# Second attention of a two-layer gated cross-attention kernel: bfloat16 maxima transposed after the value product, max rows written by DMA, parts of the next batch moved two half units ahead, sums copied by ScalarE

## What is computed

```
v = values.reshape(N, -1, HEADS, HEAD) @ Wv.T
k = keys.reshape(N, Lk, HEADS, HEAD) @ Wk.T
q = queries.reshape(N, Lq, HEADS, HEAD) @ Wq.T
energy = jnp.einsum('bqhd,bkhd->bhqk', q, k)
energy = jnp.where(mask, energy, jnp.float32(-1e+20))
attn = jax.nn.softmax(energy / np.sqrt(HEAD), axis=-1)
out = jnp.einsum('bhqk,bkhd->bqhd', attn, v).reshape(N, Lq, EMBED)
return out @ Wo.T + bo
x = x + jnp.tanh(g_xattn[1]) * _L1_xattn_ref(ctx_1024, ctx_1024, _layernorm(x, axis=-1), ...)
```

## Time and profile before

| what | value |
|---|---|
| median of three runs | 1420.08 us |
| the profiled execution's own time | 1424.06 us |
| its span, first to last instruction | 1422.3 us |
| TensorE busy | 1264.7 us, 89% |
| VectorE busy | 1044.8 us, 73% |
| ScalarE busy | 854.3 us, 60% |
| GpSimd busy | 160.5 us, 11% |
| second attention, first max product to last transposes | about 231.9 to 453 us |

### The profile page before, as it was taken

The page is one execution under the profiler, slowest core; times in us unless marked ns, Lnnn a source line. Parts: engine busy times, 40 slices in busy tenths (PEclk is TensorE's granted clock), DMA queues, the critical chain, the costliest instruction groups (busy, mean ns, idle before and its releaser), DMA issues.

```text
span 1422.3 us, 26541 instructions
## 1 busy us (share of the span) xinstructions
PE 1264.7 (89%) x10690; PEld 590.5 (42%) x10690; DVE 1044.8 (73%) x1563; ACT 854.3 (60%) x1432; POOL 160.5 (11%) x139
## 2 busy tenths in 40 slices
PE   4898974899899899948899999999999999999988
PEld 3566662454455755514433233232322333233237
DVE  4897494666664756545699999999999999999802
ACT  2233472666665155511287877887887787887871
POOL 2220021110600223310600000000000000000000
PEclk8977985999999999978799999999999999999999
DMA  5000026444450013340524443323443323443003
GB/s 177 24 1 14 1 29 111 95 85 89 90 90 2 0 67 133 134 94 11 82 50 69 82 79 57 75 54 64 82 81 62 67 56 63 82 81 48 2 1 118
DMA packets 78825, 92.56 MB, mean 65 GB/s; under 512 B 15210, under 2 KB 53356, under 8 KB 78704
## 3 DMA queue, kind: packets, MB, share of 16 engines
q1 hardware_dynamic: 78704, 90.87, 31.6%
HBM read 67.02 MB, written 23.80 MB: 64 GB/s over the span
## 4 chain that ended last, share of the span: by engine, by line
PE 58%; DVE 28%; ACT 7%; issue 4%; DMA 1%; SPq 1%; POOL 1%; DVEq 0%; ACTq 0%; POOLq 0%
DVE sm L1971 18%; PE ps L1460 9%; PE ps L1451 8%; PE ps L1432 6%; PE ps L1351 4%; ACT W L964 3%; PE ps L1216 2%; PE ps L1250 2%; PE ps L1570 2%; PE ps L1167 2%; PE ps L1358 2%; PE ps L1241 2%; PE ps L1299 1%; PE ps L1442 1%; PE ps L1387 1%
## 5 line engine op out<-in xcount | busy, mean ns | idle before, releaser
L1971 DVE TENSOR_REDUCE sm<-ps 128x1 f32<-128x1024 f32 x512 | 599.8, 1218 | 33.1 <-PE ps L1432 29.8
L964 ACT ACTIVATE W<-ps 128x512 f32<-128x512 f32 x1024 | 534.8, 604 | 140.2 <-PE ps L1460 136.3
L1460 PE MATMUL ps<-R 99*32 99x512 bf16 x4096 | 318.5, 383 | 6.2 <-ACT W L964 3.2
L1451 PE MATMUL ps<-W,R 128*32 128x512 f32 x2048 | 266.4, 596 | 0.7 <-ACT W L964 0.7
L1460 PEld LDWEIGHTS ps<-R 99*32 99x32 bf16 x4096 | 86.2, 94 | 225.4 <-ACT W L964 168.5
L882 ACT CAST R<-ps 4x2048 bf16<-4x2048 f32 x32 | 59.5, 1858 | 80.7 <-PE ps L1216 80.7
L1776 DVE TENSOR_REDUCE small<-ps 128x4 f32<-128x308 f32 x128 | 60.9, 477 | 62.6 <-PE ps L1205 62.2
L1432 PE MATMUL ps<-R 50*128 50x512 bf16 x512 | 89.2, 389 | 15.6 <-DVE sm L1971 12.9
L1432 PE MATMUL ps<-KM,R 50*128 50x512 bf16 x512 | 87.2, 384 | 9.6 <-DVE sm L1971 6.6
L1451 PEld LDWEIGHTS ps<-W,R 128*32 128x32 f32 x2048 | 63.2, 111 | 42.5 <-ACT W L964 1.4
L765 POOL COPY R<-R 128x512 f32<-128x512 f32 x16 | 10.3, 644 | 591.7 <-PE ps L1451 591.7
(11 more groups left out here) (258 smaller groups left out, 1587.1 us busy)
## 6 DMA issues: line engine op xcount, KB each, us to landing
R<-x_parts SPq DMA_DIRECT2D x96, 128.0 KB, 4.8
R<-q_parts SPq DMA_DIRECT2D x192, 64.0 KB
R<-q_parts SPq DMA_DIRECT2D x96, 128.0 KB
R<-k_parts SPq DMA_DIRECT2D x96, 128.0 KB
x_parts<-R SPq DMA_DIRECT2D x8, 768.0 KB, 4.1
q_parts<-R SPq DMA_DIRECT2D x24, 256.0 KB, 2.6
k_parts<-R SPq DMA_DIRECT2D x24, 256.0 KB, 2.6
X<-in_x SPq DMA_DIRECT2D x4, 1024.0 KB, 9.8
```

The costliest lines, as they stand in the source:

```text
L964: act.activation(PR[:, s % 2, h, :], third_bank("score", 64 * u + n), ACT.Exp, scale=0.25).then_inc(s_sfree, 1)
L1451: mm = pe.matmul(bank(7)[32 * h:32 * h + 32, :], VST[j][:, k, h, :], PR[:, s % 2, h, :], start=(k == 0), stop=(k == TB - 1))
L1460: mm = pe.matmul(o[32 * c:32 * c + 32, :], KST[j][0:MAX_ROW + 1, h, t:t + 32], QST[j][0:MAX_ROW + 1, h, 512 * (s // 8):512 * (s // 8) + 51 ...
L1971: dve.tensor_reduce(MX[:, half, h, q:q + 1], bank(2 * ((p + 1) % 2), 2), AX, ALU.max).then_inc(s_tfree, 1)
```

## The change

- `Mn` is bfloat16, and its transposes use the bfloat16 identity.
- In TensorE's order `max_transposes1(m + 2)` comes ahead of `out_transposes1(m - 2)`.
- The stack has one max row in place of four (97 rows). `K1s` has ones there, set by one memset in place of four copies from the identity. ScalarE copies the 4 x 512 maxima once, into a small buffer `mrow1` of two places, waits for that copy, and issues four DMAs, one for each head, that move one row of 512 bfloat16 each from `mrow1` into the stack. TensorE waits for these DMAs in place of the copy.
- `copy_out1` moves from VectorE's list to ScalarE's, behind the exponentials of the half unit.
- Part halves 8 to 11 are made in half units 6 to 9, and 12 to 15 in 14 to 17. The layer norm chunks before them move with them.

```diff
@@ -202,12 +202,13 @@
         XP = nc.dram_tensor("x_parts", (3, C, T), BF16).ap()
         KXP = nc.dram_tensor("ctx_key_parts", (3, C, B * KX), BF16).ap()
 
-        SR1 = SR + 4
+        SR1 = SR + 1
         K1s = R2f[0:SR1, 0:2464].bitcast(BF16).rearrange("p (h n) -> p h n", h=H)
         V1a = R2f[0:KX, 2464:4512].rearrange("p (b h d) -> p b h d", b=B, h=H)
         mb1 = R2f[0:KX, 4512:5024].bitcast(BF16)
         M1u = R2f[0:KX, 5024:5280].bitcast(U8)
         I4 = R2f[0:KX, 5280:5434].bitcast(BF16)
+        mrow1 = R2f[SR:SR + 4, 5434:5946].bitcast(BF16).rearrange("p (u n) -> p u n", u=2)
         Oe = R2f[:, 6100:7124].rearrange("p (u n) -> p u n", u=2)
         k1T = R5[:, 0:616].rearrange("p (j n) -> p j n", j=2)
         kr1 = R5[:, 616:1232].rearrange("p (j n) -> p j n", j=2)
@@ -220,7 +221,7 @@
         On = R1[:, :].rearrange("p (i c) -> p i c", i=NT)
         OnT = R3f[:, 0:2048].rearrange("p (u j n) -> p u j n", u=2, j=2)
         M1 = small[:, 400:464].rearrange("p (u q j) -> p u q j", u=2, q=8)
-        Mn = small[:, 464:528].rearrange("p (u q j) -> p u q j", u=2, q=8)
+        Mn = small[:, 464:496].bitcast(BF16).rearrange("p (u q j) -> p u q j", u=2, q=8)
         rc1 = small[:, 528:544].rearrange("p (q j) -> p q j", q=4)
         s_w1 = sem("layer1_weights_loaded")
         s_bd = sem("block_diagonals_made")
@@ -245,6 +246,7 @@
         s_mn = sem("max1_negated")
         s_mt = sem("max1_transposed")
         s_mrc = sem("max1_rows")
+        s_mrl = [sem(f"max1_rows_loaded{n}") for n in range(2)]
         s_sc = sem("scores1")
         s_e1 = sem("probs1")
         s_pv = sem("values1_product")
@@ -265,8 +267,11 @@
 
         FIRST = 4
 
+        HALVES = {max(0, 8 * (i // 4) - 2) + i % 4: FIRST + i for i in range(12)}
+        CHUNKS = {0: 3, 4: 4, 6: 5, 12: 6, 14: 7}
+
         def half_in(m):
-            return FIRST + 4 * (m // 8) + m % 8 if m % 8 < 4 and m // 8 + 1 < B else None
+            return HALVES.get(m)
 
         TURNS1 = []
         for m in range(2 * UNITS):
@@ -877,10 +882,21 @@
 
             def max_rows1(m):
                 act.wait_ge(s_mt, m + 1)
+                if m >= 2:
+                    act.wait_ge(s_mrl[m % 2], 64 * (m // 2))
+                act.copy(mrow1[:, m % 2], bank(2)[SR:SR + 4, :]).then_inc(s_mrc, 1)
                 if m >= 6:
                     act.wait_ge(s_sc, 4 * (m - 5))
-                act.copy(Xs[m // 2 % 3][SR:SR1, :, 512 * (m % 2):512 * (m % 2) + 512],
-                         bank(2)[SR:SR1, :].unsqueeze(1).to_broadcast([4, 4, 512])).then_inc(s_mrc, 1)
+                act.wait_ge(s_mrc, m + 1)
+                for j in range(4):
+                    act.dma_start(Xs[m // 2 % 3][SR:SR1, j, 512 * (m % 2):512 * (m % 2) + 512],
+                                  mrow1[j:j + 1, m % 2]).then_inc(s_mrl[m % 2], 16)
+
+            def copy_out1(m):
+                act.wait_ge(s_pv, m + 1)
+                if m >= 2:
+                    act.wait_ge(s_ot1, m - 1)
+                act.copy(Oe[:, m % 2], bank(7)).then_inc(s_oc, 1)
 
             max_rows1(0)
             max_rows1(1)
@@ -894,8 +910,11 @@
                     act.wait_ge(s_sc, n + 1)
                     act.activation(P1[:, m % 2, j, :], bank_of("score", n)[0:KX, :], ACT.Exp,
                                    scale=0.25).then_inc(s_e1, 1)
+                if m >= 1:
+                    copy_out1(m - 1)
                 if m + 2 < 2 * UNITS:
                     max_rows1(m + 2)
+            copy_out1(2 * UNITS - 1)
 
             for c in range(NC):
                 act.wait_ge(s_onT, c + 1)
@@ -1213,8 +1232,8 @@
                     pe.wait_ge(s_mrc, m)
                 for i in range(4):
 
-                    mm = pe.matmul(bank(2)[SR:SR1, P * i:P * i + P], Mn[:, m // 2 % 2, 4 * (m % 2) + i, :],
-                                   identF[:, :], start=True, stop=True)
+                    mm = pe.matmul(bank(2)[SR:SR + 4, P * i:P * i + P], Mn[:, m // 2 % 2, 4 * (m % 2) + i, :],
+                                   identB[:, :], start=True, stop=True)
                 mm.then_inc(s_mt, 1)
 
             def take_bank(what, n):
@@ -1230,7 +1249,7 @@
                 if half_in(m) is not None:
                     transpose_half(half_in(m), take_bank("half", half_in(m)))
                 b, hg = u // 4, u % 4
-                pe.wait_ge(s_mrc, m + 1)
+                pe.wait_ge(s_mrl[m % 2], 64 * (m // 2 + 1))
                 for j in range(4):
                     n = 4 * m + j
                     if u + 1 < UNITS:
@@ -1267,10 +1286,10 @@
                 scores1(m)
                 if m >= 1:
                     values1(m - 1)
+                if m + 2 < 2 * UNITS:
+                    max_transposes1(m + 2)
                 if m >= 2:
                     out_transposes1(m - 2)
-                if m + 2 < 2 * UNITS:
-                    max_transposes1(m + 2)
             values1(2 * UNITS - 1)
             out_transposes1(2 * UNITS - 2)
             out_transposes1(2 * UNITS - 1)
@@ -1763,10 +1782,7 @@
             dve.tensor_copy(I4.rearrange("p (j n) -> p j n", j=4),
                             identB[0:KX, 0:KX].unsqueeze(1).to_broadcast([KX, 4, KX])).then_inc(s_mk1, 1)
 
-            for g in range(4):
-                sel = dve.tensor_copy(K1s[SR:SR1, 4 * g:4 * g + 4, :],
-                                      identB[SR:SR1, SR:SR1].unsqueeze(2).to_broadcast([4, 4, B * KX]))
-            sel.then_inc(s_mk1, 1)
+            dve.memset(K1s[SR:SR1, :, :], 1.0).then_inc(s_mk1, 1)
             ln_chunks(2, [2], lambda c: None)
 
             def reduce1(u, qs):
@@ -1800,27 +1816,16 @@
                 dve.tensor_tensor(dst.rearrange("p q (j d) -> p q j d", j=4), O[:, :, :, 0:D],
                                   rc1.unsqueeze(3).to_broadcast([P, 4, 4, D]), ALU.mult).then_inc(s_on, 1)
 
-            def copy_out1(m):
-                dve.wait_ge(s_pv, m + 1)
-                if m >= 2:
-                    dve.wait_ge(s_ot1, m - 1)
-                dve.tensor_copy(Oe[:, m % 2], bank(7)).then_inc(s_oc, 1)
-
             maxima1(0)
             maxima1(1)
             for m in range(2 * UNITS):
                 n = half_in(m)
                 if m + 2 < 2 * UNITS:
                     maxima1(m + 2, lambda: residue(n, bank_of("half", n)) if n is not None else None)
-                if m >= 1:
-                    copy_out1(m - 1)
-
-                c = 2 * (m // 8) + {0: 3, 6: 4}.get(m % 8, NC)
-                if c < NC:
-                    ln_chunks(2, [c], lambda c: None)
+                if m in CHUNKS:
+                    ln_chunks(2, [CHUNKS[m]], lambda c: None)
                 if m >= 2:
                     normalise1(m - 2)
-            copy_out1(2 * UNITS - 1)
             normalise1(2 * UNITS - 2)
             normalise1(2 * UNITS - 1)
 
```

## The result

The changed kernel took 1479.24 us (median of 4 runs, 1469.82 to 1489.56) against 1420.03 of the kernel before in the same sessions (1418.20 to 1422.82): a ratio of 1.0417, 95% interval 1.0345 to 1.0489. The forecast of 1396.2 and its range to 1409 were wrong, and in sign. The profiled execution had a span of 1468.1 and a time of 1469.82, the fastest of the four; the medians differ by 59, the two profiled spans by 45.8. The first value product V starts at nearly the same moment (256.81, before at 257.23) and the last one at 492.75 instead of 449.60, so 43.6 of the 45.8 us arose inside the second attention.

A forecast was written before the change was run, and what follows sets the result against it. A loop through TensorE and ScalarE, both near their limit, was taken as the bound. 30 x 0.78 = 23.4, plus 1.4, minus 0.9, gave 23.9 us less: 1400.2 for the profiled execution, 1396.2 for the median; range 1386 to 1409.

The forecast's parts named there:

- the term 4i: Four row-DMA issues in ScalarE's list ahead of the next exponentials, i each, taken as 0.36 us; loop 3.52 + 4i.
- rival B: Dear issues between ScalarE's row copy and next exponential: at i = 0.60, 5.4 us lost, 1425.0 in all; chance 0.10.
- the collision: VectorE's negation blocked by GpSimd's bias additions: 6.84 us lost before, 0.9 more forecast, one negation over 3 us.
- Half units with a part: Half units that also hold h copy and residue: same ScalarE chain ahead, 0.78 us gained each, loop 6.4.
- its 4.96: Forecast loop in us between value-product starts without a part, 3.52 + 4i at i = 0.36; before, 5.74.
- the cap of 0.92 and 1.18: Most us a half unit could gain until TensorE alone bounds it: 0.92 without a part, 1.18 with one.
- Ahead of half unit 0: Max transposes before the loop, in bfloat16: 2.8 us less, about half lost again, 1.4 taken, ends 0 and 2.8.
- the slot of 0.49: ScalarE's time for the sums copy moved from VectorE, priced as one 512-element operation in a run of four.
- So this gives nothing by itself: Parts made two half units ahead: no later wait for x_parts to remove, so no gain by itself.
- Do rows come in time?: Last row DMA issued 3.07 us before its half unit needs it; 1 KB loads landed in 2.1; priced at nothing.
- rival C: Row DMAs land late beside x stacks, 1.7 us in every second half unit: 26 lost, 1422; chance 0.10.
- The figure of 50 ns: Sequencer's dispatch of a DMA by the skill text: four issues 0.2 us, giving 1388.9; not used for the sum.

The follow-up runs named there:

- e3: Changed kernel with one row DMA a half unit on ScalarE in place of four, bringing four max rows: 1405.12 us, ratio 0.9898.
- e6: Changed kernel without the row DMAs: four max rows again, written by ScalarE's 4 x 2048 cast: 1400.46 us, ratio 0.9879.
- e7: Kernel before with only its cast replaced by row copy and four row DMAs from ScalarE: 1495.76 us, ratio 1.0555.
- e1: Kernel before with only bfloat16 maxima and the max transposes ahead of the out transposes: 1411.37 us, ratio 0.9916.
- e9: Kernel before with bfloat16 maxima, the new transpose order and the moved parts; cast and VectorE sums stay: 1397.34 us, ratio 0.9837.
- e8: e1 with GpSimd's four bias additions cut into 32 pieces: 1412.95 us, ratio 0.9971.
- e5: Changed kernel with unread TensorE products: five ahead of the fourth head without a part, nine ahead of the third with one: 1453.39 us, ratio 1.0243.
- e10: e9 without VectorE's negation; the transposes multiply bfloat16 maxima with a negative identity: 1384.56 us, ratio 0.9759.
- e4: Changed kernel with five unread TensorE products ahead of the fourth head's scores only: 1488.89 us, ratio 1.0476.

## Why the prediction was wrong, point by point

- **The step that failed is the term 4i of the rows' DMAs.** "I take 0.36, the nearest row": the row was a contiguous load from HBM, as small as these, but of another kind. It was also one of the cheapest rows of that stretch: just behind it, from 43 to 55 us, the kernel before issues 24 loads of 1 KB in pieces at 0.46 to 0.57 each, for instance eight in 4.54 (`46.68 4.54 SPq L518 DMA_DIRECT2D w<-in_wk1T  x8`). Measured: 0.61 an issue, 2.53 with the gaps in place of the 1.49 assumed (4i + 0.05), on SyncE as on ScalarE. This is rival B's mechanism and almost its number (0.60; its turning point was 0.555). Its chance of 0.10 was too low: the one row of a transfer in pieces stood at 0.56, and these rows turned out to be moved in pieces as well (4096 packets on q10 for 128 transfers, 32 each). Why an issue costs 0.6 is not shown by that: e3's transfer of sixteen rows cost 0.65.
- **The same terms show that this part could not gain.** Row copy and DMAs were to cost 0.65 + 1.49 = 2.14 where the cast cost 1.88; the forecast gain came from the other parts. The prediction summed them to one loop and never set one part against what it replaced. e6 and e7 are that comparison.
- **The size of rival B was wrong by a factor of ten.** It gave 5.4 us of loss. At i = 0.61 the formula gives 5.96 a loop, 6.6 of loss over 30 half units; with the sums copy at 0.61 instead of 0.49 (0.12 x 30 = 3.6) 10.2, and 11.4 was found. This part of the model holds, within 1.2. What no case had is the 31.2 beside it: a longer ScalarE list doesn't only stretch the loop, it gathers TensorE's idle time into single waits of 1.3 and 2.3, and behind some of these the granted clock falls to 0.50. The pieces of this lay in the rows read: the prediction itself followed one wait of 2.3 into 4.5 us of lost time, but for the collision only.
- **Half units with a part** were given "the same ScalarE chain" and so about 6.4. The chain was right; they took 7.57, 0.40 more than before where 0.78 less was forecast, by the same term 4i. What had no place in the sum is that TensorE's idle time there comes in one wait of 2.3, and half of the ten falls of the clock stand at such waits.
- **Right: the way the loop is added up,** though not its 4.96. The chain from V to V closed in each kernel that could be summed: 6.13 (after), 4.83 (e6), 7.05 (e7), each to 0.01.
- **Right: the bfloat16 transposes and the order,** about as priced on TensorE (four in 0.39, the last one's passage in it), and worth 1.07 and 1.33 a loop in e1, more than the cap of 0.92 and 1.18. Where the other 0.15 comes from was not settled.
- **Ahead of half unit 0** the sum had 1.4; the first V came 0.4 earlier (256.81 against 257.23).
- **Sums on ScalarE** cost more than the slot of 0.49: 0.61, since the copy stands alone. Where rows are cast it makes the loop 4.83 (e6) instead of 4.67 (e9).
- **"So this gives nothing by itself"** (the parts two half units ahead) fails at a loop of 4.67: 11 to 14 us between e1 and e9. At 5.74 no run tests it.
- **Do rows come in time?** Predicted slack 3.07 and no wait. Mostly so: a median of 2.3 us from issue to landing, but up to 7.5, and TensorE waited twice, 4.3 us in all, each time with a fall of the clock. Under rival C this was to be 26.
- **The collision** was there, with one negation of 3.08 (forecast over 3), but that the number fits is in part luck. It ended with the second addition, not with the third as forecast, and TensorE stood 0.98 for it (at 398.57), not 3.2. In e1 (9.18) and e8 (13.11) the negation took up to four times as long. The Trainium skill (SBUF — State Buffer, "Who interferes with whom") says that such operations and GpSimd can exclude each other, and the runs agree, also for a bfloat16 result. By its rule that whoever comes first holds the shared ports for one instruction and the other waits for its end, e8 would have waited 0.7 at most; it waited 13.11, and here the measurement decides.
- **The figure of 50 ns** for the sequencer's dispatch (the Trainium skill, DMA: Bandwidth & Descriptors, "Anatomy of one DMA — SWDGE (gpsimd) path", so for DMAs that GpSimd issues) was rightly left out of the sum: 0.61 on ScalarE and 0.59 on SyncE were measured.

Why TensorE at 99% busy stayed at 0.50 for over thirty microseconds in the changed kernel, while in other places the clock came back sooner, was not settled. A wait of 2.12 in e5 was followed by no fall, so the length of a wait alone doesn't decide either. Nor was it settled why some negations get in between two additions and others do not.

## What to carry to other kernels

Before a copy is turned into DMAs, set the issues in the issuing engine's own list against the copy: here four issues of 0.61 replaced a cast of 1.86, and one issue that moved sixteen rows cost hardly more than one row's (e3), though its rows still came late at times. When an engine's list grows, ask how long TensorE will stand still in one piece, not only how much longer the loop gets, since 31.2 of the 42.6 us lost here came with those single waits and the slow clock, and not with the longer loop. Where an operation of VectorE is blocked by GpSimd, take that operation off the path (e10) rather than shorten GpSimd's instructions (e8).

## What the runs showed of the hardware that was not expected

- A DMA of one 1 KB row between two partitions takes its queue's engine about 0.6 us to issue, on ScalarE (0.611) as on SyncE (0.589), and is split into 32 packets; one that moves sixteen such rows takes 0.65 (e3).
- Products that nobody reads made the changed kernel 26 us faster (e5): the mean granted clock of the loop rose from 0.74 to 0.98. At one of the two places alone (e4, 0.87) they gained nothing.
- A VectorE operation of 16 elements a partition waited 13.11 us beside a row of 32 GpSimd additions of 0.68 each, until the last was done (e8).
